# Second attention: part of the sum over keys on TensorE, three buffers of value products, VectorE's sums two steps behind

## The chip, the cores and the metric

The kernel runs on one core of one Trainium2 chip. The metric is the device time of one execution in microseconds (us). Engines are TensorE (PE; its weight loads are listed apart as PEld), VectorE (DVE), ScalarE (ACT), GpSimd (POOL) and SyncE (SP, which only issues transfers here). SBUF is the on-chip memory, PSUM holds TensorE's results in eight banks, named `ps[0]` to `ps[7]`.

## The reference

Two transformer-like blocks on x of shape (8, 512, 256): each has a modulated layer norm, an attention and a mixture of experts. The change lies in the attention of the second block. There every token attends over its own 16 groups of 4 numbers, so scores are 16 by 16 for each row, not token by token:

```python
def shp(t):
    return t.reshape(B * G, H, -1, HD).swapaxes(1, 2)      # H = 16, HD = 4
q, k, v = (shp(q), shp(k), shp(v))
scores = q @ k.swapaxes(-2, -1) * scale
attn = jax.nn.softmax(scores, axis=-1)
o = (attn @ v).swapaxes(1, 2).reshape(B, S, dim)
return o * w.reshape(B, S, dim) @ w_out
```

Each output of `attn @ v` is a sum over 16 keys of an exponential times a value, divided by the sum of the 16 exponentials.

## The kernel before

Every engine has its own program, written out in order in one function each (`vector`, `scalar`, `gpsimd`, `tensor`, `sync`), and semaphores tie them together; nothing is scheduled automatically. The second attention is a loop over `q` from 0 to 63 (`NQ = 64`). Eight consecutive steps belong to one chunk `c = q // 8` of rows. A step handles 2 of 16 query groups for 128 partitions at once: 2 x 16 queries, 16 keys, 4 value numbers each.

What step `q` of each engine's loop does, in the order in which it stands in the program:

- **TensorE**: `less_max(q + 1)` subtracts the row maxima in PSUM (one bf16 matmul, needs VectorE's `top(q + 1)`); `project` computes the heads of a later chunk (6 fp16 matmuls of 256 columns for a head; `heads_at[q]` gives 3 heads in four steps of a chunk, 2 in one or two, 4 in a few early ones) and `turn_qk` regroups them (two turns in each of the two steps `q % 8` = 3 and 4, no heads there); `out_less`; `scores(q + 2)` sums GpSimd's products over the value dimension (4 fp32 matmuls into bank `ps[2 + q % 3]`); then, every second step, `out_project` of a finished tile, and in the others `out_turn`. TensorE starts them strictly in this order.
- **VectorE**: `top(q + 1)` (maximum over keys, L2010), `values(q, 0)` and `values(q, 1)` (exponentials times values: the first product has 16 rows of 64 numbers, of the second VectorE takes the first `vm_cut(q)` = 8 or 9 rows, L1419), `sums(q - 1)` (the sum over the 16 keys, L2032). At the end of a chunk `sums` adds a reciprocal (L2036).
- **ScalarE**: `powers(q + 1)` (exponentials into PSUM for VectorE, L2442), outputs, the copies of the heads out of PSUM (L2081), and last `powers_beside(q + 1)` (exponentials into SBUF for GpSimd and for the denominator, L2449), which waits for VectorE's sums because it writes the buffer that they read.
- **GpSimd**: `products(q + 2)` (query times key, two instructions of 1024 numbers), `values(q)` (the rows of the second product that VectorE leaves), and once a chunk `divide` and `weigh`, all on L2547.

The value products of a step lie in `PV[q % 2]`, laid out `[2 products, 16 queries, 5, 16 keys]`; the five are the 4 value numbers and the exponential itself. `sums` reduces all of it: 160 sums of 16, 2560 numbers read. The heads and the turns share two PSUM banks, `ps[0]` and `ps[1]`, in turn; `pj_free(n)` makes TensorE wait until ScalarE has copied the unit that last used the bank. `vr` counts finished sums, `vm` and `vm_p` finished value products of VectorE and GpSimd, `e_sb` the finished `powers_beside`, `qk` and `qt` the copies of heads and turns.

Of the kernel before, what the change touches and what calls it, by code (L numbers as in the profile page):

```python
# [71 lines left out]
def program(nc, x_in, wqk_in, wv_in, wo_in, rw_in, rb_in, w1_in, w3_in, w2_in, c0_in, m0_in,  # L72
# [3 lines left out]
    with ctx:  # L76
# [428 lines left out]
        def head_unit(c, h):  # L505
            return 12 + 20 * (c - 1) + h if c else h // 2
# [66 lines left out]
        def vm_cut(q):  # L573
            return (8 if q < 16 else 9) if q < 61 else 0
# [250 lines left out]
        def tensor(e):  # L825
# [446 lines left out]
            def pj_free(n):  # L1272

                if n >= 14:
                    c, h = 1 + (n - 14) // 20, (n - 14) % 20
                    if h < 16:
                        pe.wait_ge(s["qk"], heads_copied(c, h))
                    else:
                        pe.wait_ge(s["qt"], 4 * c + h - 15)
                elif n >= 10:  # L1280
                    pe.wait_ge(s["qt"], n - 9)
                elif n >= 2:
                    pe.wait_ge(s["qk"], heads_copied(0, 2 * (n - 2)))
# [131 lines left out]
        def vector(e):  # L1415
# [596 lines left out]
            def values(q, r):  # L2012
# [8 lines left out]
                tt(PV[q % 2][:, r, 0:n, 0:4, :], bc(et[:, 0:n], 2, 4), v[:, 0:n], ALU.mult).then_inc(s["vm"], 1)

            def sums(q):
# [27 lines left out]
            for q in range(NQ):  # L2051
# [25 lines left out]
        def scalar(e):  # L2077
# [342 lines left out]
            def turn_qk(c, bs):  # L2420
                for b in bs:
# [491 lines left out]
```

## Time and profile before

| | us |
|---|---|
| median of 3 runs (1740.03 to 1744.47) | 1744.17 |
| the profiled execution, its own time | 1743.46 |
| its span in the profile | 1741.7 |
| the second attention's loop (first `top` to last sum) | 1082.1 to 1448.2 |

How to read it: the profile covers one execution, 1.8 us of whose time lie outside the span. The loop of the second attention is 366 us of it, with little other work in it but the output tiles of the same attention. A row of the profile's timeline gives start and length; on VectorE and GpSimd records overlap by some tenths of a microsecond, so the time that an instruction takes from its engine is read from one start to the next.

### The profile page before, as it was taken

The numbers are of one execution on the slowest core, as the hardware profiler recorded it, in microseconds if no ns is written. First come the engines' busy times: TensorE is split into PE (matmuls) and PEld (weight loads), VectorE is DVE, ScalarE is ACT, GpSimd is POOL, SyncE is SP. The second block draws the span as 40 slices with busy tenths as digits, with TensorE's granted clock in tenths as the row PEclk, the third lists the DMA queues.
The fourth block names the chain that finished last, engine by engine and source line by source line (L and its number), as shares of the span: only waits on it lengthen the run. The fifth ranks groups of instructions, "written<-read, shape, count | busy, mean of one in ns | idle before, by whom it ended". The sixth has DMA issues, their size and how long they took to land.

```text
span 1741.7 us, 38208 instructions
## 1 busy us (share of the span) xinstructions
PE 1529.0 (88%) x13596; PEld 1145.4 (66%) x13596; DVE 1119.5 (64%) x1777; ACT 909.7 (52%) x2313; POOL 1221.5 (70%) x1024
## 2 busy tenths in 40 slices
PE   6799999986999999999999967877877767699998
PEld 5456666565788888888888853433333326599997
DVE  6778898887334434434444557899999998533332
ACT  5768888853343443433444346545555536344553
POOL 4647777743376776776777727999999996466664
PEclk9899999996799999999999977889999978599999
DMA  6003444419245445444465461011111246388885
GB/s 219 20 30 119 142 135 139 124 35 326 77 96 122 112 108 122 110 110 119 101 186 151 107 188 53 1 28 31 31 43 43 91 152 194 141 259 253 259 262 150
DMA packets 148049, 217.34 MB, mean 125 GB/s; under 512 B 48904, under 2 KB 108576, under 8 KB 142752
## 3 DMA queue, kind: packets, MB, share of 16 engines
q1 hardware_dynamic: 115296, 132.26, 23.6%
q0 software_dynamic: 32576, 82.63, 19.4%
q8 instruction: 122, 2.00, 0.5%
q14 instruction: 55, 0.45, 0.1%
HBM read 143.23 MB, written 71.61 MB: 123 GB/s over the span
## 4 chain that ended last, share of the span: by engine, by line
PE 54%; POOL 20%; DVE 8%; issue 7%; DMA 5%; ACT 1%; POOLq 0%; DVEq 0%; ACTq 0%; SPq 0%
PE ps L829 51%; POOL BIG L2547 16%; DMA BIG<-HB,BIG 5%; DVE BIG L1419 4%; PE ps L946 1%; POOL BIG L2731 1%; POOL BIG L2732 1%; POOL XD L2721 1%; DVE BIG L2032 1%; PE ps L1127 1%; ACT BIG L2081 1%; DVE bnst L1426 1%; POOL BIG L2709 1%; PE ps L1196 0%; POOL out L2721 0%
## 5 line engine op out<-in xcount | busy, mean ns | idle before, releaser
L829 PE MATMUL ps<-BIG 128*128 128x256 f16 (+9 forms) x11168 | 1230.7, 285 | 122.8 <-DVE BIG L2010 49.2
L829 PEld LDWEIGHTS ps<-BIG 128*128 128x128 f16 (+3 forms) x11168 | 940.9, 100 | 382.4 <-DVE BIG L2010 77.8
L2547 POOL TENSOR_TENSOR BIG<-BIG 128x256 f16<-128x256 f32 (+7 forms) x550 | 728.5, 1499 | 221.8 <-ACT BIG L2081 207.6
L2081 ACT ACTIVATE BIG<-BIG 128x512 f16<-128x512 f32 (+3 forms) x527 | 318.1, 661 | 225.5 <-DVE BIG L1419 160.5
L1419 DVE TENSOR_TENSOR BIG<-BIG 128x512 f16<-128x512 f32 (+12 forms) x345 | 258.6, 758 | 209.7 <-ACT BIG L2081 166.6
L2081 ACT ACTIVATE BIG<-ps 128x64 f32<-128x64 f32 (+7 forms) x663 | 232.1, 424 | 210.0 <-PE ps L1127 114.1
L1419 DVE TENSOR_TENSOR BIG<-ps,BIG 128x512 f32<-128x512 f32 (+3 forms) x389 | 285.3, 811 | 13.9 <-PE ps L829 12.5
L1419 DVE TENSOR_TENSOR BIG<-BIG,ps 128x512 f32<-128x512 f32 (+2 forms) x149 | 95.6, 642 | 185.9 <-PE ps L829 160.7
L2032 DVE TENSOR_REDUCE BIG<-BIG 128x160 f32<-128x2560 f32 x64 | 186.5, 2915 | 0.0
L2721 POOL DMA_INDIRECT XD<-BIG x67 | 113.2, 1690 | 85.2 <-DVE BIG L1916 81.4
L2709 POOL DMA_INDIRECT BIG<-HB,BIG x106 | 113.4, 1070 | 50.6 <-issue 26.4
L2155 ACT ACTIVATE BIG<-ps,BIG 128x64 f32<-128x64 f32 x480 | 101.7, 363 | 49.5 <-PE ps L829 49.5
L2721 POOL DMA_INDIRECT out<-BIG x39 | 62.7, 1607 | 60.2 <-DVE BIG L1951 57.6
L2342 ACT ACTIVATE BIG<-ps 128x512 f32<-128x512 f32 x78 | 46.7, 598 | 104.2 <-PE ps L829 98.2
L2295 ACT ACTIVATE BIG<-ps 128x512 f32<-128x512 f32 (+1 forms) x140 | 79.9, 571 | 24.2 <-PE ps L829 20.1
L2731 POOL DMA_INDIRECT BIG<-PT,BIG x67 | 68.3, 1019 | 20.5 <-issue 20.5
L2732 POOL DMA_INDIRECT BIG<-GT,BIG x67 | 66.1, 986 | 20.4 <-issue 20.4
L1916 DVE SCALAR_TENSOR_TENSOR BIG<-ps,BIG 128x256 f32<-128x256 f32 x67 | 32.4, 484 | 71.9 <-PE ps L829 71.7
L2449 ACT ACTIVATE BIG<-ps 128x512 f32<-128x512 f32 x64 | 38.3, 599 | 76.3 <-DVE BIG L2032 76.3
L2442 ACT ACTIVATE ps<-ps 128x512 f32<-128x512 f32 x64 | 37.2, 581 | 54.0 <-PE ps L829 53.8
L829 PE MATMUL ps<-BIG,tri 128*128 128x512 f16 (+1 forms) x264 | 63.1, 377 | 0.9 <-ACT BIG L2108 0.9
L2010 DVE TENSOR_REDUCE BIG<-ps 128x32 bf16<-128x512 f32 x64 | 48.1, 752 | 20.4 <-PE ps L829 20.2
(175 smaller groups left out, 1018.6 us busy)
## 6 DMA issues: line engine op xcount, KB each, us to landing
WD<-BIG SPq DMA_DIRECT2D x80, 256.0 KB
BIG<-in_v SPq DMA_DIRECT2D x32, 512.0 KB
BIG<-in_w SPq DMA_DIRECT2D x24, 512.0 KB
BIG<-WD SPq DMA_DIRECT2D x32, 384.0 KB, 7.7
HB<-BIG SPq DMA_DIRECT2D x64, 128.0 KB, 2.5
WG<-BIG SPq DMA_DIRECT2D x32, 256.0 KB
BIG<-WD SPq DMA_DIRECT2D x16, 512.0 KB, 5.0
XD<-X SPq DMA_DIRECT2D x32, 128.0 KB, 2.5
```

The lines of the kernel that those rows point to most:

```text
L829: return e.matmul(o, lhsT, rhs, start=start, stop=stop, skip_group_check=True)
L1419: return e.tensor_tensor(o, a, b, op)
L2010: e.tensor_reduce(SM[q % 4], shaped(ps[2 + q % 3][:, :], (2, 16, 16)), AX.X, ALU.max).then_inc(s["sm"], 1)
L2032: e.tensor_reduce(OB[c % 2][:, 2 * q2:2 * q2 + 2], PV[q % 2], AX.X, ALU.add).then_inc(s["vr"], 1)
L2081: return e.activation(o, i, ACT.Copy)
L2155: o = e.activation(KVF[i % 2][:, j, 512 + 64 * h:576 + 64 * h], ps[4 + vr_no["v", i, 1] % 2][:, 64 * h:64 * h + 64], ACT.Copy, scale=q[:, ...
L2295: e.activation(m_.UP[u % 2][:, 0:w], ps[2 * u % 4][:, 0:w], ACT.Silu).then_inc(s["su"], 1)
L2547: return e.tensor_tensor(o, a, b, op)
L2709: e.indirect_dma_start(m_.HIN[t % ring], None, m_.HB, bass.IndirectOffsetOnAxis(m_.gi[:, t:t + 1], 0)).then_inc(ld_hi[t % ring], 16)
L2721: e.indirect_dma_start(m_.XD, bass.IndirectOffsetOnAxis(m_.yi[:, t:t + 1], 0), m_.YO[t % 2], None, compute_op=ALU.add).then_inc(st_y[t % 2 ...
L2731: e.indirect_dma_start(m_.PP[:, t:t + 1], None, PT, bass.IndirectOffsetOnAxis(m_.qi[:, t:t + 1], 0)).then_inc(ld_g[t % 3], 16)
L2732: e.indirect_dma_start(m_.G[t % 3], None, GT, bass.IndirectOffsetOnAxis(m_.bi[:, t:t + 1], 0)).then_inc(ld_g[t % 3], 16)
```

## The change

TensorE sums the last 3 or 4 of the 16 keys of a step (3 where it has more than 2 heads to compute in the next step, else 4) with as many fp32 matmuls by the identity, 160 columns each, into the ring `ps[0]`, `ps[1]`. ScalarE copies the 160 sums into the slot of the first of these keys. VectorE's reduction then reads 17 - 3 or 17 - 4 numbers for each sum instead of 16. This holds for steps below `N_SUM = 58`. There is a third buffer of value products, in the space of a weight that is no longer used (`WM1`), `sums` runs two steps behind (`sums(q - 2)`), with two sums in step 60 to catch up, and GpSimd's `divide` and `weigh` move one step later. VectorE takes 11 (first ten steps) or 12 rows of the second product until step 57, GpSimd the other 5 or 4.

```diff
+        PV.append(shaped(WM1.rearrange(FLAT)[:, 0:2560], (2, 16, 5, 16)))
...
+        N_SUM = 58
+        s["ks_ps"], s["ks"] = s["gt"], s["gt_ps"]
+
+        def keys_by_pe(q):
+            if q >= N_SUM:
+                return 0
+            return 3 if len(heads_at[q + 1]) > 2 else 4
+
+        def late_keys(q):
+            return PV[q % 3].rearrange("p r f d k -> p k (r f d)")
+
+        in_turns = [("two", 0, 2 * j) for j in range(8)] + [("turn", 0, b) for b in range(4)]
+        for q in range(NQ):
+            in_turns += [("head", c, h) for c, h in heads_at[q]]
+            in_turns += [("turn", q // 8 + 1, b) for b in turns_next(q)]
+            in_turns += [("keys", q - 1, 0)] if 0 < q <= N_SUM else []
+        unit = {u: n for n, u in enumerate(in_turns)}
+
+        def sums_at(q):
+
+            return {N_SUM + 2: (q - 2, q - 1)}.get(q, (q - 1,) if q > N_SUM + 2 else (q - 2,))
...
-            return (8 if q < 16 else 9) if q < 61 else 0
+            return (11 if q < 10 else 12) if q < N_SUM else 9 if q < 61 else 0
...
+            def sum_keys(q):
+                if not 0 <= q < N_SUM:
+                    return
+                n, first = unit["keys", q, 0], 16 - keys_by_pe(q)
+                pj_free(n)
+                pe.wait_ge(s["vm"], vm_n[q])
+                pe.wait_ge(s["vm_p"], q + 1)
+                pe.wait_ge(s["e_sb"], q + 1)
+                for k in range(first, 16):
+                    m = mm(ps[n % 2][:, 0:160], ident[:, :], late_keys(q)[:, k], k == first, k == 15)
+                m.then_inc(s["ks_ps"], 1)
...
                 turn_qk(q // 8 + 1, turns_next(q))
+                sum_keys(q - 1)
                 for n in out_at(q, O_OUT):
                     out_less(n)
...
-                if q >= 2:
-                    dve.wait_ge(s["vr"], q - 1)
+                if q >= 3:
+                    dve.wait_ge(s["vr"], q - 2)
...
-                e.tensor_reduce(OB[c % 2][:, 2 * q2:2 * q2 + 2], PV[q % 2], AX.X, ALU.add).then_inc(s["vr"], 1)
+                keys, by_pe = 16, keys_by_pe(q)
+                if by_pe:
+                    dve.wait_ge(s["ks"], 1 + q + 1)
+                    keys = 17 - by_pe
+                e.tensor_reduce(OB[c % 2][:, 2 * q2:2 * q2 + 2], PV[q % 3][:, :, :, :, 0:keys], AX.X, ALU.add).then_inc(s["vr"], 1)
...
-                sums(q - 1)
+                for last in sums_at(q):
+                    sums(last)
...
+            def sum_keys(q):
+                if not 0 <= q < N_SUM:
+                    return
+                act.wait_ge(s["ks_ps"], 1 + q + 1)
+                copy(late_keys(q)[:, 16 - keys_by_pe(q)], ps[unit["keys", q, 0] % 2][:, 0:160]).then_inc(s["ks"], 1)
...
-                if q % 8 == 1 and q > 8:
+                if q % 8 == 2 and q > 8:
                     divide(q // 8 - 1)
-                if q % 8 == 2 and q > 8:
+                if q % 8 == 3 and q > 8:
                     weigh(q // 8 - 1)
```

On TensorE, a step with three heads and no projection stood like this before; `sm` is VectorE's `top`, `pm` GpSimd's products, the rows of 128x256 are the heads, those of 32x512 the scores:

```order
L829 MATMUL ps<-BIG 128x512 [waits sm]
L829 MATMUL ps<-BIG 128x256 [waits qk]
L829 MATMUL ps<-BIG 128x256 x5
L829 MATMUL ps<-BIG 128x256 [waits qk]
L829 MATMUL ps<-BIG 128x256 x5
L829 MATMUL ps<-BIG 128x256 [waits qk]
L829 MATMUL ps<-BIG 128x256 x5
L829 MATMUL ps<-BIG 32x512 [waits e_sb,pm]
L829 MATMUL ps<-BIG 32x512 x3
```

Such a step in the changed kernel; `gt_ps` is the semaphore that counts ScalarE's copies of the key sums, the rows of 128x160 are the sums over keys:

```order
L852 MATMUL ps<-BIG 128x512 [waits sm]
L852 MATMUL ps<-BIG 128x256 [waits qk]
L852 MATMUL ps<-BIG 128x256 x5
L852 MATMUL ps<-BIG 128x256 [waits gt_ps]
L852 MATMUL ps<-BIG 128x256 x5
L852 MATMUL ps<-BIG 128x256 [waits qk]
L852 MATMUL ps<-BIG 128x256 x5
L852 MATMUL ps<-BIG,ident 128x160 [waits vm_p,e_sb,vm,qk]
L852 MATMUL ps<-BIG,ident 128x160 x2
L852 MATMUL ps<-BIG 32x512 [waits pm]
L852 MATMUL ps<-BIG 32x512 x3
```

The three matmuls of the key sum now stand between the heads and the scores of the same step, and the second head waits for ScalarE's copy of the key sum of the step before.

On VectorE, steps 60 and 61 before:

```order
L2010 TENSOR_REDUCE BIG<-ps3 128x32 [waits mx_ps,s_ps]
L1419 TENSOR_TENSOR BIG<-ps5,BIG 128x16x64 [waits vr,e_ps]
L1419 TENSOR_TENSOR BIG<-ps5,BIG 128x9x64
L2032 TENSOR_REDUCE BIG<-BIG 128x160 [waits e_sb,vm_p,vm]
L2010 TENSOR_REDUCE BIG<-ps4 128x32 [waits mx_ps,s_ps]
L1419 TENSOR_TENSOR BIG<-ps7,BIG 128x16x64 [waits vr,e_ps]
L2032 TENSOR_REDUCE BIG<-BIG 128x160 [waits e_sb,vm_p,vm]
```

And in the changed kernel (L2045 is the maximum, L1454 the products, L2071 the sum over keys):

```order
L2045 TENSOR_REDUCE BIG<-ps3 128x32 [waits mx_ps,s_ps]
L1454 TENSOR_TENSOR BIG<-ps5,BIG 128x16x64 [waits vr,e_ps]
L1454 TENSOR_TENSOR BIG<-ps5,BIG 128x9x64
L2071 TENSOR_REDUCE BIG<-BIG 128x160 [waits e_sb,vm_p,vm]
L2071 TENSOR_REDUCE BIG<-WM1 128x160 [waits e_sb,vm_p,vm]
L2045 TENSOR_REDUCE BIG<-ps4 128x32 [waits mx_ps,s_ps]
L1454 TENSOR_TENSOR BIG<-ps7,BIG 128x16x64 [waits vr,e_ps]
L2071 TENSOR_REDUCE BIG<-BIG 128x160 [waits e_sb,vm_p,vm]
```

The sums of steps 58 and 59 both stand in step 60 now, with all 16 keys, ahead of the maximum that step 61 begins with.

## Rows read from the trace of the kernel before

**Rows 1.** Busy time: stretch, its us, PE, PEld, DVE, ACT, POOL, granted clock.

```profile
1182.60:1226.10 43.50, 34.84 (x252) 16.72 (x252) 43.05 (x35) 25.23 (x100) 43.50 (x27) 1.00 0.12 31
...
1270.90:1315.60 44.70, 35.70 (x252) 17.14 (x252) 43.05 (x35) 25.32 (x101) 44.70 (x27) 0.96 0.15 42
...
sum 223.10, PE 173.04 PEld 79.95 DVE 215.85 ACT 121.36 POOL 223.10; mean PE 34.61 PEld 15.99 DVE 43.17 ACT 24.27 POOL 44.62
```

**Rows 2.** Timeline of DVE, one regular step (start us, us, engine line op, shapes, count).

```profile
1253.62 0.88 DVE L2010 TENSOR_REDUCE BIG<-ps 128x32 bf16<-128x512 f32 x1
1254.21 2.08 DVE L1419 TENSOR_TENSOR BIG<-ps,BIG 128x1024 f32<-128x1024 f32 x2
1256.01 3.00 DVE L2032 TENSOR_REDUCE BIG<-BIG 128x160 f32<-128x2560 f32 x1
1258.74 0.87 DVE L2010 TENSOR_REDUCE BIG<-ps 128x32 bf16<-128x512 f32 x1
```

**Rows 3.** Timeline of DVE at the end of a chunk.

```profile
1269.27 1.76 DVE L2036 RECIPROCAL BIG<-BIG 128x256 f32<-128x256 f32 x1
1270.94 0.63 DVE L2010 TENSOR_REDUCE BIG<-ps 128x32 bf16<-128x512 f32 x1
```

**Rows 4.** Timeline of POOL in the same steps, three starts.

```profile
1249.66 3.45 POOL L2547 TENSOR_TENSOR BIG<-BIG 128x1024 f32<-128x1024 f32 x2
...
1251.63 3.45 POOL L2547 TENSOR_TENSOR BIG<-BIG 128x448 f32<-128x448 f32 x2
...
1252.73 2.35 POOL L2547 TENSOR_TENSOR BIG<-BIG 128x1024 f32<-128x1024 f32 x1
```

**Rows 5.** Timeline of PE, steps with turns, after GpSimd's divide and weigh.

```profile
1237.65 2.32 PE L829 MATMUL ps<-BIG,ident 32*32 32x512 f32 x16
1241.91 1.41 PE L829 MATMUL ps<-BIG 128*32 128x512 f32 x8 [1.94 <-POOL BIG L2547]
```

**Rows 6.** Who waited for whom, 1270.9 to 1315.6 (us, times, longest).

```profile
PEld ps L829 <- POOL BIG L2547: 5.1, 4, 4.1
```

**Rows 7.** Timeline of PE, one step with three heads and a projection.

```profile
1253.16 0.71 PE L829 MATMUL ps<-ident,BIG 128*128 128x128 f32 x4
1254.55 1.70 PE L829 MATMUL ps<-BIG 128*128 128x512 bf16 x13 [0.69 <-DVE BIG L2010]
1256.57 0.83 PE L829 MATMUL ps<-BIG 128*128 128x256 f16 x6 [0.32 <-ACT BIG L2081]
...
1257.44 1.83 PE L829 MATMUL ps<-BIG 128*32 128x512 f32 x14
...
1259.67 3.66 PE L829 MATMUL ps<-BIG 128*128 128x512 bf16 x27
```

**Rows 8.** Timeline of PE: the last of the four fp32 records.

```profile
1253.59 0.28 PE L829 MATMUL ps<-ident,BIG 128*128 128x128 f32 x1
```

**Rows 9.** Timeline of PE, two steps with four heads, and one with turns.

```profile
1119.13 5.90 PE L829 MATMUL ps<-BIG 128*128 128x512 bf16 x33 [0.81 <-DVE BIG L2010]
1125.85 4.12 PE L829 MATMUL ps<-BIG 128*128 128x512 bf16 x33 [0.82 <-DVE BIG L2010]
...
1108.55 0.39 PE L829 MATMUL ps<-BIG 128*128 128x512 bf16 x1 [0.93 <-DVE BIG L2010]
1108.87 2.32 PE L829 MATMUL ps<-BIG,ident 32*32 32x512 f32 x16
1111.12 1.07 PE L829 MATMUL ps<-BIG 128*32 128x512 f32 x8
```

**Rows 10.** Timeline of DVE, the maximum between those two steps with four heads.

```profile
1125.10 0.69 DVE L2010 TENSOR_REDUCE BIG<-ps 128x32 bf16<-128x512 f32 x1 [1.57 <-PE ps L829]
```

**Rows 11.** Busy time in the two stretches of the 33 matmuls (PEclk: granted clock).

```profile
1119.50:1124.00 4.50, 4.50 (x29) 3.19 (x29) 4.03 (x3) 2.11 (x10) 4.50 (x4) 0.61 0.02 4
1126.00:1130.10 4.10, 3.97 (x33) 2.25 (x31) 4.10 (x3) 2.61 (x13) 4.10 (x4) 1.00 0.00 0
```

**Rows 12.** Timeline of DVE, the maximum of step 62.

```profile
1433.42 0.69 DVE L2010 TENSOR_REDUCE BIG<-ps 128x32 bf16<-128x512 f32 x1 [1.11 <-PE ps L829]
```

More of the change, by code:

```diff
@@ L505, in head_unit @@
         def head_unit(c, h):
-            return 12 + 20 * (c - 1) + h if c else h // 2
+            return unit["head", c, h] if c else h // 2
         def heads_copied(c, h):
@@ L1272, in pj_free @@
             def pj_free(n):
[L1274 to L1283, printed above, removed]
+                if n < 2:
+                    pe.wait_ge(s["gw"], 4)
+                    return
+                kind, c, h = in_turns[n - 2]
+                if kind == "turn":
+                    pe.wait_ge(s["qt"], 4 * c + h + 1)
+                elif kind == "keys":
+                    pe.wait_ge(s["ks"], 1 + c + 1)
                 else:
-                    pe.wait_ge(s["gw"], 4)
+                    pe.wait_ge(s["qk"], heads_copied(c, h))
             def project(c, h):
@@ L1305, in turn_qk @@
                 for b in bs:
-                    n = 20 * c - 8 + 16 + b
+                    n = unit["turn", c, b]
                     pe.wait_ge(s["qk"], heads_copied(c, 15))
@@ L1347, in out_turn @@
                 elif n == N_IN:
+                    pe.wait_ge(s["ks"], 1 + N_SUM)
                     pe.wait_ge(s["qk"], heads_copied(7, 15))
@@ L2427, in turn_qk @@
                         act.wait_ge(s["pm"], pm_p[8 * (c - 2) + 7])
-                    copy(QT[c % 2][:, b].rearrange("p s f h -> p (s f h)"), ps[b % 2][:, :]).then_inc(s["qt"], 1)
+                    copy(QT[c % 2][:, b].rearrange("p s f h -> p (s f h)"), ps[unit["turn", c, b] % 2][:, :]).then_inc(s["qt"], 1)
             def powers(q):
@@ L2446, in powers_beside @@
                     return
-                if q >= 2:
-                    act.wait_ge(s["vr"], q - 1)
-                e.activation(PV[q % 2][:, :, :, 4, :], shaped(ps[2 + q % 3][:, :], (2, 16, 16)),
+                if q >= 3:
+                    act.wait_ge(s["vr"], q - 2)
+                e.activation(PV[q % 3][:, :, :, 4, :], shaped(ps[2 + q % 3][:, :], (2, 16, 16)),
                              ACT.Exp, scale=0.5).then_inc(s["e_sb"], 1)
@@ L2493, in scalar @@
                 turn_qk(q // 8 + 1, turns_next(q))
+                sum_keys(q - 1)
                 for n in out_at(q, O_OUT):
@@ L2827, in values @@
                 pool.wait_ge(s["e_sb"], q + 1)
-                if q >= 2:
-                    pool.wait_ge(s["vr"], q - 1)
+                if q >= 3:
+                    pool.wait_ge(s["vr"], q - 2)
                 v = VT[q // 8 % 3].rearrange("p (f d) k -> p f d k", d=4)
-                tt(PV[q % 2][:, 1, n:16, 0:4, :], bc(PV[q % 2][:, 1, n:16, 4, :], 2, 4), v[:, n:16], ALU.mult).then_inc(s["vm_p"], 1)
+                tt(PV[q % 3][:, 1, n:16, 0:4, :], bc(PV[q % 3][:, 1, n:16, 4, :], 2, 4), v[:, n:16], ALU.mult).then_inc(s["vm_p"], 1)
             def divide(c, part=0):
```

3 lines of the change are left out of this document (2 added, 1 removed).

## The prediction, made blind

> **What bounds the kernel now.** I read the busy table by chunk first. In the five chunks between 1182.6 and 1405.7 GpSimd is busy all of 223.1 us and VectorE 215.9 of them; TensorE shows 173.0 [rows 1]. So two engines are full and a third has a margin that must be read more closely, because the change gives it work.
>
> The timeline of VectorE shows a regular step: maximum at 1253.62, products at 1254.21, sums at 1256.01, next maximum at 1258.74 [rows 2]. That is 0.59 + 1.80 + 2.73 = 5.12 us without a gap. At the end of a chunk comes a reciprocal; from one maximum to the next that step takes 5.12 + 1.96 (the sums begin at 1266.25, 2.73 later would come the next maximum, it comes at 1270.94; in the rows the reciprocal begins at 1269.27 and takes 1.67 of it [rows 3]). Eight steps and a reciprocal are 42.9 us. The chunk in rows 1 took 44.70. The other 1.8 us are one wait: after `divide` and `weigh` GpSimd's products come late, TensorE stands before the scores until 1241.91 [rows 5], and VectorE behind it. The list of waits has TensorE's weight loads waiting for GpSimd for 5.1 us, 4.1 of it in one piece [rows 6]. The chunk before the first of these waits took 43.50 [rows 1], which is the same step without most of it.
>
> **VectorE's part.** The sums read 2560 numbers in 2.73 us, 1.07 ns each. With 3 keys on TensorE they read 2240, with 4 they read 2080: -0.34 and -0.51 us. The products read 1600 numbers in 1.80 us, 1.12 ns each; 3 more rows of 64 cost +0.21 [rows 2]. So a step needs 4.99 or 4.82 us, and a chunk, which has four of each, 1.7 less than before.
>
> **GpSimd's part.** A product takes 1.97 us (1249.66 to 1251.63), its 7 rows of values 1.10 (1251.63 to 1252.73) [rows 4]. Four rows lie between 0.63 (in proportion) and 0.81 (on the line through both); I take 0.72. That is 0.38 less in each step, 3.0 in a chunk, against the 4 us of `divide` and `weigh`. GpSimd needs 5.0 - 0.4 = 4.66 a step, less than VectorE, and the third buffer with `divide` a step later costs it no more than before. I expect the one wait of 1.8 us to go.
>
> If that were all, a chunk would take 44.7 - 1.7 - 1.8 = 41.2 us.
>
> **TensorE's part.** The key sum stands between the heads and the scores. There is a closed loop here: the maximum waits for the scores, `less_max` for the maximum, and the heads, the key sum and the next scores follow in order on TensorE. Its length can be read where it already bound: a run of 33 matmuls (`less_max`, four heads, scores) begins at 1119.13 and takes 5.90, to 1125.03; VectorE's maximum starts at 1125.10, the next `less_max` at 1125.85 [rows 9, 10]. So a step can't be shorter than 0.75 + the run + 0.07. What that gives before the change:
> - Three heads with a projection: `less_max` at 1254.55, scores at 1257.44, and scores last 1.07 [rows 7, 9]: run 3.96, loop 4.78 against the 5.12 that VectorE needs. Slack 0.34.
> - Three heads after a projection: `less_max` comes 0.93 after the maximum (1259.67 less 1258.74) because the projection is still running, run 3.66 [rows 2, 7]: 4.66, slack 0.46.
> - Two turns: 1108.55 to 1111.12, plus 1.07 [rows 9]: run 3.64, loop 4.46, and up to 0.3 more with a projection before it or `out_less` in it.
>
> Price of the key sum: the profile shows an fp32 matmul as two records. Four records of 128 columns start between 1253.16 and 1253.59, 0.143 apart [rows 7, 8]. The trace has none of 160 columns. If the records are not bound by their columns, a matmul costs 2 x 0.143 = 0.29; in proportion to columns it costs 0.36. I take 0.29, because 128 columns are much nearer to 160 than to nothing and the spacing of short records holds a part that does not grow: 0.86 for three keys, 1.15 for four; 0.36 stays as the other end.
>
> The Trainium skill gives another price. "FP8 and Floating Point Precision", section TensorE Precision Notes, says that true FP32 takes four passes through the array; at 2.4 GHz, 160 columns would be an estimated 0.27 us a matmul, 0.80 and 1.07 for a key sum, and by it the chunk below would be 0.4 us shorter. No row here has the width to decide it.
>
> New loops: three heads 4.78 + 0.86 = 5.64 and 4.66 + 0.86 = 5.52, instead of 5.12. Both runs contain waits for ScalarE's copies of the heads (0.32 in the row at 1256.57 [rows 7]); now that VectorE finishes before the loop does, ScalarE starts a step's work earlier against TensorE, so some of it falls away. I take 5.45. Turns: 5.61 to 5.9, taken as 5.75. The step `q % 8` = 2 has two heads and a projection: 3.96 less 0.66 for a head (6 of the matmuls at about 0.11), 1.15 and 0.82 more, 5.3 with the ScalarE wait and 4.95 without it, 5.0. The step `q % 8` = 1 has the reciprocal now and stays VectorE's: 4.99 + 1.95 = 6.94. Sum of a chunk: 4 x 5.45 + 2 x 5.75 + 5.0 + 6.94 = 45.2, against 44.7. Nearly all that VectorE and GpSimd gain goes to TensorE's loop.
>
> **The whole loop.**
> - Steps 24 to 47, three chunks: about 0.4 more each, +1.
> - Steps 16 to 23 had next to no wait for GpSimd to lose: 45.2 against 43.5, +1.7.
> - Steps 0 to 15: four-head steps become 4.94 + 0.86 = 5.8 where they took 5.06, four times +0.75. Against that, the series of matmuls of 5.90 us came after a wait, at a granted clock of 0.61, where the same series at 1.00 took 4.12 [rows 9, 11]; one or two such steps get 1 to 1.8 shorter. Together +1.5.
> - Steps 48 to 55: heads end at step 50, three steps are VectorE's at 4.82: -1.3.
> - Steps 56 to 59: no heads, VectorE's at 4.8, and the last wait for GpSimd goes: -2.5.
> - Steps 60 to 63: the doubled sums bring +2.73, of which the wait of 1.11 in step 62 [rows 12] and some others take up half: +1.2.
>
> Sum +1.6 us. With the lower price of the key sum, or with ScalarE's waits gone altogether, it is -3. I take -1. The profiled execution, 1743.46, is 0.7 below the median; from the median 1744.17 this is 1743 us. A difference under 0.3%, 5 us, can't be told from none here.
>
> ScalarE gets one copy of 160 columns, about what it pays for a copy of a head, ahead of `powers_beside`; that one waited for VectorE's sums anyway. The copy and the reduction that reads it are a step apart. Cover gone, it costs 0.3 us a step.
>
> **The rivals.**
> 1. VectorE stays the bound: TensorE's runs shrink, by ScalarE's waits and a cheap key sum, below 4.99. For it: TensorE's busy time is only 35.7 of 44.7 in a chunk [rows 1]. Against it: the busy share says nothing of a loop with 0.3 to 0.5 us slack that gets 0.86. Halfway there (loops of 5.2 and 5.5, chunk 43.9) six chunks give -8, 1735 us; all the way, 41.2 a chunk, about -20, 1724.
> 2. Slower: the key sum costs 0.36 us a matmul, in proportion to its columns, and ScalarE's waits stay. Three heads 5.8, turns 6.0, the two-head step 5.5: with 6.94 a chunk is 47.6. Against 44.7 that is +2.9 over the four and a half chunks in which heads are computed, 1757 us. It decides from 0.32 us a matmul on. For it: the records at 1253.16 and after include weight loads that wider columns may not hide.
> 3. The clock: TensorE's waits for GpSimd go, and with them the stretches at half clock (1.2 GHz); the granted clock was 0.96 over the chunk in rows 1. A mean of 0.96 means 8% of the chunk, 3.6 us, at half clock, so up to 1.8 us of TensorE's time a chunk comes back, and as TensorE's loop is now the bound, it shows: 45.2 - 1 a chunk, -5 more, 1737 us. The Trainium skill, "TensorE: Matmul & The Clock Gate", Part 1: The HAM clock gate, says that the default state is throttled and that activity releases it, so a busier TensorE should run warmer; rows 11 agree on the two levels. Against it: the series at half clock lie right behind the waits, mostly in steps that had slack or that I have counted.
> 4. The new copy holds up ScalarE, and `powers_beside` becomes late: +0.3 a step in 58 steps, 1760. Little speaks for it, as ScalarE is busy 25 of 44.7 us.
>
> **Chances.** My forecast 0.42, of which 0.06 ends above +5 us; rival 1 0.22; rival 3 0.14; rival 2 0.16; rival 4 0.04; 0.02 for no effect at all. Faster by over 0.3% comes from rivals 1 and 3: 0.36. Slower: rivals 2 and 4 and 0.06 of the first, 0.26. Within 0.3%: 0.38. The forecast's own range is 1738 to 1750; taken out to rival 1 short of VectorE's bound and to rival 2 it is 1729 to 1756.
>
> **What would show it.** The 128x160 fp32 records on TensorE give the price: 3 of them 0.86, 4 of them 1.15 from the start of the first to the start of the scores. The maximum should wait for TensorE in most steps, three-head steps should be 5.4 to 5.5 apart, the turn steps 5.7 to 5.8; the sums should take 2.4 and 2.2. GpSimd should have gaps, and its wait of 1.9 at the scores should be gone. I am wrong if the maxima stand 4.8 to 5.0 apart in three-head steps: then VectorE is still the bound.

## The result, and the profile after

| | median us | ratio to before, 95% interval |
|---|---|---|
| before, 5 runs (1740.03 to 1744.47) | 1741.35 | |
| after, 5 runs (1804.29 to 1808.71) | 1805.29 | 1.037 [1.0356, 1.0383] |
| predicted | 1743 (1729 to 1756) | |

The changed kernel is slower by 3.7%, far above the predicted range. Its profiled execution took 1808.56 us, with a span of 1806.8. The whole loss lies in the second attention: from the first maximum to the last the loop takes 418.6 us (1080.09 to 1498.71) where it took 351.3 (1082.09 to 1433.42), 67.3 more, against 65.1 in the span.

The page of the profile after: busy time, the chain that ended last, and three of the costliest groups.

```profile
PE 1635.2 (91%) x14006; PEld 1224.2 (68%) x14006; DVE 1107.0 (61%) x1777; ACT 928.4 (51%) x2371; POOL 1195.5 (66%) x1024
...
PE 69%; DVE 11%; POOL 6%; issue 4%; DMA 4%; ACT 3%; POOLq 0%; DVEq 0%; ACTq 0%; SPq 0%
...
L852 PE MATMUL ps<-BIG,ident 128*128 128x160 f32 (+1 forms) x534 | 125.1, 779 | 6.8 <-ACT BIG L2121 6.1
...
L2071 DVE TENSOR_REDUCE BIG<-BIG 128x160 f32<-128x2080 f32 (+2 forms) x43 | 105.9, 2462 | 0.0
...
L2045 DVE TENSOR_REDUCE BIG<-ps 128x32 bf16<-128x512 f32 x64 | 43.8, 684 | 97.1 <-PE ps L852 97.1
```

The last row is the one to read first. Ahead of the maxima VectorE now stands idle for 97.1 us over the 64 steps, all of it put down to TensorE. TensorE has 69% of the chain that ended last, where it had 54% before.

One chunk (eight steps) in the busy table, the one that answers to the 44.70 us of [rows 1]:

```profile
core 0: us, PE busy (x) PEld busy (x) DVE busy (x) ACT busy (x) POOL busy (x), PEclk, DMA share, GB/s
1299.36:1354.07 54.71, 51.85 (x310) 28.48 (x309) 42.18 (x33) 27.98 (x108) 42.26 (x26) 0.94 0.13 35
```

A chunk takes 54.7 us, ten more. VectorE and GpSimd have become lighter, as the change meant; TensorE, with 35.7 us before, shows 51.9. The timeline of TensorE in two three-head steps, which answer to [rows 7], the first without and the second with `out_less`:

```profile
1342.60 2.66 PE L852 MATMUL ps<-BIG 128*128 128x512 bf16 x19
1345.09 1.78 PE L852 MATMUL ps<-BIG,ident 128*128 128x160 f32 x6
1346.81 1.06 PE L852 MATMUL ps<-BIG 128*32 128x512 f32 x8
1347.80 0.71 PE L852 MATMUL ps<-ident,BIG 128*128 128x128 f32 x4
1348.69 2.58 PE L852 MATMUL ps<-BIG 128*128 128x512 bf16 x19 [0.17 <-DVE BIG L2045]
1351.11 1.79 PE L852 MATMUL ps<-BIG,ident 128*128 128x160 f32 x6
```

Three key-sum matmuls are six records of 160 columns, from 1345.09 until the scores start at 1346.81: 1.72 us where 0.86 was forecast. Record by record the starts are 0.271 us apart, so a matmul costs 0.54 us and not 0.29. VectorE's timeline over these steps:

```profile
1341.64 0.69 DVE L2045 TENSOR_REDUCE BIG<-ps 128x32 bf16<-128x512 f32 x1 [3.23 <-PE ps L852]
1342.25 2.08 DVE L1454 TENSOR_TENSOR BIG<-ps,BIG 128x1024 f32<-128x1024 f32 x2
1344.25 2.31 DVE L2071 TENSOR_REDUCE BIG<-WM 128x160 f32<-128x2080 f32 x1
1347.94 0.69 DVE L2045 TENSOR_REDUCE BIG<-ps 128x32 bf16<-128x512 f32 x1 [1.38 <-PE ps L852]
```

VectorE is through long before the next maximum may start: 6.30 us a step (1341.64 to 1347.94), 1.38 of them waiting, against 5.12 without a gap in [rows 2]. The sums over keys cost what the prediction said (2.31 for 2080 numbers).

The turn steps lost most, they take 8.45 and 8.58 us now. TensorE in the first, and behind the dots the key sum of the second:

```profile
1325.58 0.38 PE L852 MATMUL ps<-BIG 128*128 128x512 bf16 x1
1325.89 2.22 PE L852 MATMUL ps<-BIG,ident 32*32 32x512 f32 x16
1328.71 2.42 PE L852 MATMUL ps<-BIG,ident 128*128 128x160 f32 x8 [0.61 <-ACT BIG L2121]
1331.06 1.93 PE L852 MATMUL ps<-BIG 128*32 128x512 f32 x8
...
1337.40 2.42 PE L852 MATMUL ps<-WM,ident 128*128 128x160 f32 x8 [0.70 <-ACT BIG L2121]
```

And ScalarE, which copies the turns:

```profile
1328.06 1.09 ACT L2121 ACTIVATE BIG<-ps 128x512 f32<-128x512 f32 x2 [1.11 <-PE ps L852]
```

Three things stand in these rows. The key sum follows two turns in the ring of two banks, so it waits for ScalarE's copy of the first turn, and that copy starts only at 1328.06, when TensorE is done with both. The key sum then takes 2.35. And the scores, which take 1.07 in [rows 9], take 1.93 here, with the granted clock down to 0.50, the 1.2 GHz level (PEclk, the third number from the end):

```profile
1328.71:1331.05 2.34, 2.34 (x8) 1.53 (x8) 0.99 (x1) 0.44 (x1) 2.34 (x2) 0.96 0.76 196
1331.06:1333.07 2.01, 2.01 (x10) 0.34 (x9) 0.01 (x1) 1.65 (x6) 1.60 (x2) 0.50 0.75 177
...
1337.40:1339.90 2.50, 2.50 (x9) 2.05 (x9) 1.01 (x1) 0.48 (x2) 0.08 (x1) 0.56 0.00 0
```

### The profile page after: what moved, and what is told of

The parts are those of the page before. It is cut to its first block, busy times and chain, and to the rows that moved or that the text cites. A ratio compares the mean times of both kernels' runs of the same rounds, so it can differ in the third digit from the quotient of the medians.

```text
span 1806.8 us, 39194 instructions
## 1 busy us (share of the span) xinstructions
PE 1635.2 (91%) x14006; PEld 1224.2 (68%) x14006; DVE 1107.0 (61%) x1777; ACT 928.4 (51%) x2371; POOL 1195.5 (66%) x1024
## 4 chain that ended last, share of the span: by engine, by line
PE 69%; DVE 11%; POOL 6%; issue 4%; DMA 4%; ACT 3%; POOLq 0%; DVEq 0%; ACTq 0%; SPq 0%
PE ps L852 66%; DVE BIG L1454 4%; DMA BIG<-HB,BIG 3%; POOL BIG L2594 3%; ACT BIG L2121 2%; DVE BIG L2071 2%; PE ps L969 1%; DVE BIG L2045 1%; PE ps L1150 1%; POOL XD L2768 1%; ACT ps L2482 1%; POOL BIG L2778 1%; POOL BIG L2779 1%; DVE bnst L1461 1%; POOL BIG L2756 0%
## 5 line engine op out<-in xcount | busy, mean ns | idle before, releaser
L2594 POOL TENSOR_TENSOR BIG<-BIG 128x256 f16<-128x256 f32 (+7 forms) x529 | 691.6, 1336 | 279.6 <-ACT BIG L2121 213.6
L1454 DVE TENSOR_TENSOR BIG<-BIG 128x512 f16<-128x512 f32 (+12 forms) x345 | 256.0, 750 | 210.0 <-ACT BIG L2121 167.9
L2121 ACT ACTIVATE BIG<-ps 128x64 f32<-128x64 f32 (+8 forms) x702 | 250.6, 425 | 258.4 <-PE ps L852 116.6
L1454 DVE TENSOR_TENSOR BIG<-ps,BIG 128x512 f32<-128x512 f32 (+2 forms) x348 | 248.8, 781 | 13.8 <-PE ps L852 12.4
L1454 DVE TENSOR_TENSOR BIG<-BIG,ps 128x512 f32<-128x512 f32 (+2 forms) x149 | 95.7, 642 | 189.7 <-PE ps L852 159.4
L852 PE MATMUL ps<-BIG,ident 128*128 128x160 f32 (+1 forms) x534 | 125.1, 779 | 6.8 <-ACT BIG L2121 6.1
L2071 DVE TENSOR_REDUCE BIG<-BIG 128x160 f32<-128x2080 f32 (+2 forms) x43 | 105.9, 2462 | 0.0
L2045 DVE TENSOR_REDUCE BIG<-ps 128x32 bf16<-128x512 f32 x64 | 43.8, 684 | 97.1 <-PE ps L852 97.1
L2382 ACT ACTIVATE BIG<-ps 128x512 f32<-128x512 f32 x78 | 46.6, 598 | 104.1 <-PE ps L852 100.7
L852 PEld LDWEIGHTS ps<-BIG,ident 128*128 128x128 f32 (+1 forms) x534 | 59.6, 165 | 48.4 <-ACT BIG L2121 31.6
```

Of the source, the lines that this page charges most:

```text
L852: return e.matmul(o, lhsT, rhs, start=start, stop=stop, skip_group_check=True)
L1454: return e.tensor_tensor(o, a, b, op)
L2045: e.tensor_reduce(SM[q % 4], shaped(ps[2 + q % 3][:, :], (2, 16, 16)), AX.X, ALU.max).then_inc(s["sm"], 1)
L2071: e.tensor_reduce(OB[c % 2][:, 2 * q2:2 * q2 + 2], PV[q % 3][:, :, :, :, 0:keys], AX.X, ALU.add).then_inc(s["vr"], 1)
L2121: return e.activation(o, i, ACT.Copy)
L2594: return e.tensor_tensor(o, a, b, op)
```

## The experiments

The question was why the same fp32 matmul that showed 0.143 us a record for 128 columns [rows 8] took 0.271 for 160. What differs besides the width is how the moving operand lies in SBUF: the key sum reads one key of `[16 queries, 5, 16 keys]`, 160 numbers 64 bytes apart. Theory A says that the step costs TensorE half its rate. The kernel before ran again beside each experiment, with medians from 1736.85 to 1744.87, so only ratios to it are compared. Step and chunk times are worked out from the starts of the maxima; a chunk is the fifth, steps 32 to 39, unless another is named.

**e1_close: TensorE reads the same amount, adjacent.** This kernel, e4_strides, e5_keys_turns and e7_close_after leave the last 3 or 4 keys out of the attention.

```diff
-            return PV[q % 3].rearrange("p r f d k -> p k (r f d)")
+            return ...rearrange("p (k n) -> p k n", k=16) if by == "pe" else ...
```

> The changed kernel, but TensorE's key sum reads 160 numbers that lie next to each other instead of 160 that lie 64 bytes apart (other numbers of the same buffer), and ScalarE multiplies its copy by 0, so the last 3 or 4 keys are missing from the attention. Number and size of all instructions stay. Theory A (the 64 byte step halves the rate at which TensorE reads the moving operand): records of the key sum 0.13 to 0.14 us apart instead of 0.27, a chunk 28 x 2 x 0.135 = 7.6 us shorter, 54.7 to 47.1, time about 1755. Theory B (each fp32 record pays for its weight load on top of its columns): records stay at 0.27, time stays at 1805.

Measured: ratio 1.0088 [1.0068, 1.0108]. Records 0.136 apart instead of 0.271. TensorE in a turn step:

```profile
1296.61 1.35 PE L852 MATMUL ps<-BIG,ident 128*128 128x160 f32 x8 [0.51 <-ACT BIG L2121]
1297.89 1.07 PE L852 MATMUL ps<-BIG 128*32 128x512 f32 x8
```

Its chunk and its scores in the busy table:

```profile
1269.93:1316.43 46.50, 42.58 (x310) 24.54 (x309) 42.11 (x33) 28.90 (x109) 41.86 (x26) 1.00 0.14 41
1297.89:1299.03 1.14, 1.14 (x10) 0.30 (x10) 0.01 (x1) 1.03 (x4) 1.14 (x2) 1.00 0.83 214
```

Theory A holds, and time and chunk are as expected: one changed step of one operand gives back 8.2 of the 10 us a chunk, 1.4 of them by way of the clock (worked out below). In this chunk the granted clock stays at 1.00 and the scores take 1.07 again, though the engine waits nearly as long ahead of the key sum. It doesn't stay there everywhere: one turn step of the chunk of steps 16 to 23 took 8.15 us, and there eight adjacent records took as long as strided ones:

```profile
1208.43 2.50 PE L852 MATMUL ps<-BIG,ident 128*128 128x160 f32 x8 [0.66 <-ACT BIG L2121]
```

```profile
1208.43:1210.73 2.30, 2.30 (x9) 2.18 (x9) 1.14 (x1) 0.44 (x1) 2.20 (x2) 0.50 0.00 0
```

**e4_strides: 4, 8, 16 and 32 bytes in successive chunks.** One run, as e1_close otherwise.

```diff
+            step = (1, 2, 4, 8)[q // 8 % 4]
+            return ...[:, 0:160 * step * (16 // step)].rearrange("p (k n s) -> p k n s", n=160, s=step)[:, :, :, 0]
```

> As the run with adjacent numbers (ScalarE's copy times 0), but the step of the 160 numbers that TensorE reads is 4, 8, 16 and 32 bytes in chunks 0 and 4, 1 and 5, 2 and 6, 3 and 7. Theory A: records 0.13 apart at 4 bytes and 0.27 from some step on, which the run is to tell. Theory B: 0.27 in all chunks.

Measured: 1774.94 us in one run. TensorE's key sums of four keys at 4, 8, 16 and 32 bytes:

```profile
1109.74 1.35 PE L855 MATMUL ps<-BIG,ident 128*128 128x160 f32 x8 [0.50 <-ACT BIG L2124]
...
1144.80 1.40 PE L855 MATMUL ps<-BIG,ident 128*128 128x160 f32 x8
...
1186.14 2.51 PE L855 MATMUL ps<-BIG,ident 128*128 128x160 f32 x8
...
1241.48 2.56 PE L855 MATMUL ps<-BIG,ident 128*128 128x160 f32 x8
```

Medians of the spacing between records are 0.136, 0.142, 0.284 and 0.290 us (0.271 at 64 bytes in the changed kernel). Between 8 and 16 bytes the spacing doubles, and beyond it hardly changes: a cliff and not a slope. That 64 bytes came out a little cheaper than 32 is not explained.

**e2_kmajor: keys outermost in the buffer, everything computed.**

```diff
-        PV = area.ring(2, 2, 16, 5, 16)
+        PV = area.ring(2, 16, 2, 16, 5)
...
+        PV = [v.rearrange("p k r f d -> p r f d k") for v in PV]
```

> The changed kernel with the value products laid out with the key outermost ([16 keys, 2, 16, 5] in memory instead of [2, 16, 5, 16 keys]); everything computed as before. TensorE then reads 160 adjacent numbers, VectorE, ScalarE and GpSimd write with a step of 640 bytes and VectorE's sum reads with that step. Theory A: records 0.13 to 0.14 apart and about 1755, if the other engines do not care for the step. Theory B: 1805. A third result: the other engines pay for the step, VectorE's sum longer than 2.3 to 2.5 us, and the time over that of the run with adjacent numbers and scrap data.

Measured: ratio 1.0825 [1.0793, 1.0857], the third of the results that the expectation names. TensorE's records are 0.136 apart for the most part, but VectorE's groups became dear, against 2476 ns for the same sum after the change, and TensorE waited for it:

```profile
L2072 DVE TENSOR_REDUCE BIG<-BIG 128x160 f32<-128x2240 f32 x17 | 69.9, 4113 | 0.0
```

```profile
1320.48:1383.60 63.12, 48.62 (x308) 27.36 (x308) 62.55 (x35) 31.35 (x108) 43.43 (x26) 0.89 0.11 30
```

The step that was taken from TensorE was given to VectorE, 640 bytes between two keys, and VectorE pays as well: sums of 2240 numbers 4.1 us instead of 2.5, products of 1024 numbers 2.10 instead of 1.26.

**e3_no_pe: three buffers and the lag alone.** No key sum, VectorE's rows as before.

```diff
-            if q >= N_SUM:
-                return 0
+            return 0
             return 3 if len(heads_at[q + 1]) > 2 else 4
...
-            return (11 if q < 10 else 12) if q < N_SUM else 9 if q < 61 else 0
+            return (8 if q < 16 else 9) if q < 61 else 0
```

> Three buffers, sums two steps behind, divide and weigh a step later, but no key sum on TensorE and none on ScalarE, VectorE's sums over all 16 keys and its 8 or 9 rows of the second product as in the kernel before. If the key sum is the whole loss: VectorE bound at 5.12 a step, 1738 to 1745, with GpSimd's wait of 1.9 a chunk at most partly gone because GpSimd needs 5.04 a step as before. If the lag or the third buffer costs by itself: 1750 or more.

Measured: ratio 0.9995 [0.9983, 1.0008]. This part is neutral, so the loss comes with the key sum. The wait for GpSimd's products stayed, in smaller pieces:

```profile
PEld ps L850 <- POOL BIG L2589: 3.7, 5, 1.5
```

Against 5.1 us, 4.1 of it at once [rows 6]. The doubled sums make one step at the end 7.85 us long (5.13 before), but the next and the one ahead of it get shorter.

**e5_keys_turns: e1_close with the key sum ahead of the turns.**

```diff
-                turn_qk(q // 8 + 1, turns_next(q))
                 sum_keys(q - 1)
+                turn_qk(q // 8 + 1, turns_next(q))
```

> As the run with adjacent numbers (same part of the keys left out), but in the two steps of a chunk with turns the key sum stands ahead of the turns instead of behind them, on TensorE and ScalarE. Theory: behind the turns the key sum waits for ScalarE's copy of the first turn, which starts only when both turns are done; ahead of them it waits for nothing. Turn steps 5.7 us instead of 6.5, 13 or so of them: 1744 against 1754.5. Rival: the turn steps are long because of the turns and the key sum themselves: 1754.

Measured: ratio 1.0051 [1.0033, 1.0069]; turn steps 6.35 where e1_close had 6.52 and 6.58. The expectation of 5.7 failed. The wait for a copy changed its place: by the order in the ring the second turn now needs the copy of the key sum, and from the start of the turns to the scores it takes 2.72 us instead of the 2.25 of [rows 9].

**e6_after_scores: the changed kernel with the key sum behind the scores.** Everything computed, 64-byte step.

```diff
-                sum_keys(q - 1)
                 for n in out_at(q, O_OUT):
                     out_less(n)
                 if q:
                     scores(q + 2)
+                sum_keys(q - 1)
```

> The changed kernel with the key sum behind the scores instead of ahead of them (ScalarE's copy behind its copy for the output). All is computed. Theory: the loss lies in the closed loop from scores to maximum to less_max, not in TensorE's total; about 0.9 us behind the scores were idle in every second step and the turn steps' wait for ScalarE falls there too. Three-head steps alternate around 5.3 and 6.2 instead of 6.13 and 6.30, turn steps 5.3 to 6.5 instead of 8.5: 1755 to 1765. If TensorE's total were the bound instead, the place would not matter: 1805.

Measured: ratio 1.0225 [1.0204, 1.0246], chunk 51.58. The direction is right (3.1 us a chunk less than after), the size was overestimated. The turn steps came near what was expected (6.80 and 6.47 for an expected 5.3 to 6.5, instead of 8.45 and 8.58) and the two-head step fell from 6.03 to 4.83, but the three-head steps, expected at 5.3 and 6.2, took 6.4 to 6.9, more than the 6.1 to 6.3 after the change. With TensorE busy 48.8 of the 51.6 us the engine itself is nearly full, so little more is to be had by moving work inside its program.

```profile
1280.85:1332.43 51.58, 48.76 (x309) 28.36 (x310) 42.07 (x34) 27.44 (x108) 41.66 (x27) 1.00 0.13 37
```

**e7_close_after: both, adjacent and behind the scores.** The edits of e1_close and e6_after_scores.

> Both: adjacent numbers (last 3 or 4 keys left out, ScalarE's copy times 0) and the key sum behind the scores. 0.8 us of key sum fit into the 0.9 us in which TensorE waits for the maximum, so steps without projection are VectorE's at 4.8 to 5.0, those with one 5.0 to 5.3; a chunk 42 to 43.5: 1725 to 1735, faster than the kernel before. If ScalarE's later copy or the buffer ring holds it up: 1740 or more.

Measured: ratio 0.9983 [0.9969, 0.9997], below the expected gain; it is the other outcome that the expectation names, a hold-up by ScalarE's copy. Turn steps fell to 5.2 and the two-head step to 4.76, but three-head steps stayed at 5.59 to 5.90: TensorE's loop sets them still, and in it stands a wait for ScalarE ahead of the third head:

```profile
1299.30 0.83 PE L852 MATMUL ps<-BIG 128*128 128x256 f16 x6 [0.98 <-ACT BIG L2121]
```

**e8_rows10: e3_no_pe with 10 rows for VectorE.**

```diff
-            return (8 if q < 16 else 9) if q < 61 else 0
+            return 10 if q < 61 else 0
```

> No key sum, three buffers and sums two steps behind, and VectorE takes 10 rows of the second product in all steps below 61 (before 8 or 9), GpSimd 6. All is computed. Theory: with 5.04 us a step plus 4 a chunk GpSimd sets the chunk's 45 us; VectorE 5.19 a step and 43.5 a chunk, GpSimd 4.92 a step: the chunk 43.6, time 1728 to 1732. Rival: VectorE is the bound already: 61 rows of 0.07, 1741.

Measured: ratio 0.997 [0.9958, 0.9982], between the two expectations; steps 5.19, and one of 6.00 a chunk; chunks 44.1 to 44.7 in the middle of the loop. The step of 6.00 does not wait for GpSimd. It is the one behind the reciprocal: TensorE has stood idle for 3.58 us for VectorE's maximum, the granted clock is 0.50 in the whole step, the 13 matmuls take 3.17 us where they take 1.70 in [rows 7], and the next maximum waits 0.79 us for the scores:

```profile
1275.44 3.17 PE L850 MATMUL ps<-BIG 128*128 128x512 bf16 x13 [3.58 <-DVE BIG L2041]
1280.75 0.69 DVE L2041 TENSOR_REDUCE BIG<-ps 128x32 bf16<-128x512 f32 x1 [0.79 <-PE ps L850]
```

```profile
1274.75:1280.75 6.00, 5.31 (x23) 2.28 (x24) 5.21 (x5) 2.76 (x10) 5.83 (x4) 0.50 0.00 0
```

**e9_some_keys: the key sum only where VectorE is late.** Everything computed, 64-byte step, 4 keys in one step of eight and in the headless end.

```diff
-            return 3 if len(heads_at[q + 1]) > 2 else 4
+            return 4 if (q + 1) % 8 == 1 or q >= 52 else 0
...
+            return (11 if q % 8 in (2, 3, 4) else 10) if q < 61 else 0
```

> The changed kernel, all of it computed, with TensorE's key sum (of 4 keys) only in one step of eight, the one behind the turns' last, and in the headless end, and VectorE at 11 rows in the three steps behind it and 10 elsewhere below step 61. Theory A (a key-sum matmul at a 64-byte step costs TensorE 0.54 us, and it pays only where TensorE had a wait to give): one step a chunk takes 8 x 0.54 = 4.3 us more of TensorE; put where VectorE is late, it costs a chunk nothing and lets VectorE and GpSimd catch up some 0.6 to 1.1 us a chunk, chunks of 43.3 to 43.8 us beside 44.4 without any key sum: ratio 0.993 to 0.995. Rival (TensorE has no free 4.3 us even there): chunks of 45 us or more, ratio 0.998 to 1.005.

Measured: ratio 0.9958 [0.9944, 0.9972]. The chunk takes 43.83, about as expected. The step of 6.00 in e8_rows10 takes 4.70, but not for the reason that the expectation gives, work taken from VectorE and GpSimd alone: 0.50 of the difference is VectorE's sum of 2080 instead of 2560 numbers (2.31 and 2.81 us), and 0.79 is the wait for TensorE, which is gone. The key sum fills a part of the time in which TensorE stood idle, 1.02 us are left of the 3.58, and the granted clock is 1.00:

```profile
1275.01 1.70 PE L853 MATMUL ps<-BIG 128*128 128x512 bf16 x13 [1.02 <-DVE BIG L2046]
```

```profile
1274.33:1279.02 4.69, 4.00 (x30) 2.25 (x30) 4.69 (x5) 2.06 (x9) 4.54 (x4) 1.00 0.01 3
```

No run fills the gap without lightening the sum, so the two parts are read from the rows and not tested apart. The ratio falls a little short of what was expected, and its interval overlaps that of e8_rows10 (0.9958 to 0.9982 there), so the gain of 4.1 us between the two loops (348.6 and 344.5 from first to last maximum) is seen in the profiles and not settled by the times.

```profile
1256.58:1300.41 43.83, 38.47 (x266) 18.82 (x265) 43.72 (x34) 25.90 (x101) 43.68 (x28) 0.96 0.14 43
```

**e10_two_keys: 2 keys in every step.**

```diff
-            return 3 if len(heads_at[q + 1]) > 2 else 4
+            return 2
```

> The changed kernel, all of it computed, with TensorE summing 2 keys in every step instead of 3 or 4. Theory A (0.54 us a matmul, TensorE's loop sets the step): 28 x 2 = 56 matmuls a chunk of eight steps become 32, a run is 1 to 2 heads x 2 fewer; per step 3 or 4 keys x 2 halves = 6 or 8 matmuls become 4, so 2 to 4 fewer, about 24 a chunk x 0.27 us a record pair's half or 0.54 a matmul: 6.5 us a chunk at least, from 54.7 to about 48, time about 1762 (ratio 1.010 to 1.015). Rival (what costs is the key sum's being there at all, its wait for the power copies and ScalarE's copy behind it): little changes, 1790 or more, ratio above 1.027.

Measured: ratio 1.0233 [1.0216, 1.025], between the two expectations. Three-head steps take 5.59 and 5.76 where they took 6.13 and 6.31: 0.54 and 0.55 for the one matmul fewer. The rest falls short, because VectorE with 12 rows and 15 numbers needs 5.15 (two-head step 5.09 instead of 6.03, 0.94 for two matmuls; in four other chunks that step took 5.73 to 5.91, at a mean granted clock of 0.70), and because of turn steps like the second of these, where the scores of the same program ran at a lower granted clock:

```profile
1258.41:1259.55 1.14, 1.14 (x10) 0.30 (x10) 0.00 (x1) 1.03 (x4) 1.14 (x2) 1.00 0.94 230
1306.22:1307.96 1.74, 1.74 (x10) 0.28 (x9) 0.00 (x0) 1.59 (x6) 1.74 (x2) 0.59 0.87 221
```

The first turn step of the chunk was 6.50 us in the one case and 7.11 in the other, 0.6 apart, and the scores show all of it.

**e11_pairs: two keys adjacent, an 8-byte step for TensorE, everything computed.** Three keys on TensorE in every step, VectorE three of four value numbers of the second product.

```diff
-        PV = area.ring(2, 2, 16, 5, 16)
+        PV = area.ring(2, 8, 2, 5, 16, 2)
...
+            return PV[q % 3].rearrange("p r d f a b -> p a b (r d f)")
...
+                    m = mm(ps[n % 2][:, 0:160], ident[:, :], late_keys(q)[:, k // 2, k % 2], k == first, k == 15)
```

> The changed kernel, all of it computed, with the value products laid out in pairs of keys: eight pairs outermost, and inside each the 160 numbers with their two keys adjacent. TensorE then reads one key at a step of 8 bytes; VectorE and GpSimd write and read two adjacent numbers and then step 1280 bytes. TensorE sums 3 keys in every step, VectorE takes three of the four value numbers of the second product (as much as 12 rows) below step 61, and ScalarE writes the exponentials for GpSimd in two instructions instead of one. Theory (an operand runs at full rate if two reads in a row fall within 16 bytes, on TensorE and on VectorE): key-sum records 0.142 us apart, VectorE's sums of 2240 numbers 2.4 to 2.6 us as before, chunks 45.5 to 46.5 us, ratio 1.003 to 1.010. Rival (what VectorE pays for is any large step inside the operand, also when two numbers are adjacent): sums of 3.9 us and more, chunks above 55 us, ratio above 1.05.

Measured: ratio 1.0121 [1.0097, 1.0146], two thousandths above the expected end; the chunk is 47.6 us, 1.1 above the expected 46.5. The mechanism is as expected on both engines: records 0.142 us apart, and VectorE reads pairs 1280 bytes apart at the old price:

```profile
L2072 DVE TENSOR_REDUCE BIG<-BIG 128x160 f32<-128x2240 f32 x24 | 59.9, 2496 | 0.0
```

2496 ns beside 4113 in e2_kmajor and 2476 after the change. The miss lies in the turn steps again, 6.11 and 7.87 in this chunk. In the second the scores ran at 0.50 granted clock:

```profile
1302.00:1304.30 2.30, 2.30 (x11) 0.33 (x10) 0.00 (x0) 1.17 (x4) 1.79 (x2) 0.50 0.00 0
```

**e12_pairs_after: the same, with the key sum behind the scores.** The edit of e6_after_scores.

> The kernel with pairs of keys, all of it computed, with the key sum behind the scores instead of ahead of them. Theory (with the cheap read TensorE's loop is the last bound, and behind the scores the key sum leaves the part of the loop that the maximum waits for): the turn steps fall to 5.2 to 5.4 us and the step behind them to 4.8 to 5.1, chunks of 44.5 to 45.5 us, ratio 0.996 to 1.001. Rival (the order doesn't matter once the read is cheap): the same as with the key sum ahead of the scores, within 0.2%.

Measured: ratio 0.9978 [0.9967, 0.9989], as expected, with turn steps of 5.0 and a two-head step of 4.93. This is the whole change with its read mended and its key sum moved, and it is faster than before, by 0.2%. What holds it is one wait in each three-head step, here in the last row, 0.97 us ahead of the third head:

```profile
1249.47:1294.21 44.74, 40.95 (x301) 23.90 (x302) 42.04 (x33) 27.67 (x116) 41.77 (x27) 1.00 0.15 42
```

```profile
1256.36 1.69 PE L853 MATMUL ps<-BIG 128*128 128x512 bf16 x13
1259.02 0.83 PE L853 MATMUL ps<-BIG 128*128 128x256 f16 x6 [0.97 <-ACT BIG L2122]
```

The bank of that head is not emptied by ScalarE in time. Three-head steps take 5.6 to 5.9.

## Why the prediction was wrong

**The step that failed** is the price of the key sum: "I take 0.29 ... 0.36 stays as the other end." Measured: 0.54 us a matmul, beyond both ends. The number 0.143 was read from matmuls whose moving operand, the identity, is adjacent; I weighed width against width and never asked how the 160 numbers lie. The diff says it, in `rearrange("p r f d k -> p k (r f d)")`, a step of 16 numbers. The upper bound was taken on the wrong property. e1_close and e4_strides show this step alone to be the cause of the doubled price, and e10_two_keys shows the price by the dose. Of the 3.7% e1_close gives back 2.8 (1.037 to 1.0088); most of the rest lies in the turn steps, below.

The Trainium skill states the rule, in "Advanced Engine Details and Errata", section SBUF Cachelines: lines are 16 bytes, and at least two reads must fall on one line for full performance. The runs agree: 8 bytes full rate, 16 bytes half (0.142 and 0.284 us), and with pairs VectorE full rate again. The prediction cited another page of the Trainium skill, whose four passes for true FP32 made an estimated 0.27 us a matmul ("FP8 and Floating Point Precision", TensorE Precision Notes); with adjacent numbers that is what the runs show, 2 x 0.136.

The prediction's own sum of a chunk, beside the fifth chunk:

| steps | predicted | after | e1_close |
|---|---|---|---|
| four with three heads, each | 5.45 | 6.22 | 5.41 |
| two with turns, together | 11.5 | 17.03 | 13.1 |
| the one with two heads | 5.0 | 6.03 | 4.97 |
| the one with the reciprocal | 6.94 | 6.79 | 6.79 |
| chunk | 45.2 | 54.7 | 46.5 |

- **The loop** "0.75 + the run + 0.07" was right, and so were its lengths: with the key sum at 0.27 a matmul (e1_close) three of the four rows come out within 0.15. Rival 2 named the right place and direction; its 0.36 and its 1757 us were too small by the same error.
- **Turn steps** had a second error: the 1.6 us between 11.5 and 13.1 are there without the strided read. Each waits for ScalarE's copy of the first turn (0.51 to 0.70 us on TensorE), since the key sum is the third user of two banks. The prediction counted that wait for heads only. Those waits are 1.1 to 1.3 of the 1.6; the rest isn't resolved. What lies between 13.1 and 17.0 is 8 matmuls by 0.27, 2.2, and the lower clock, 0.87 in one step and 0.54 in the other (from the scores to the maximum 2.00 and 1.67 instead of 1.13), 3.6 of 3.9. That the strided read itself brings the lower clock on is not shown.
- **VectorE and GpSimd** were right: sums of 2.48 and 2.3 us, 4.82 in the steps without heads, the reciprocal step 6.79, GpSimd 42.3 of 54.7 us a chunk. GpSimd's wait at the scores went as forecast: TensorE's waits for it in the chunk are 1.6 us, the longest 0.4, where they were 5.1 and 4.1.
- **The third rival, the clock**, did not come to pass where it was priced: TensorE became busier (35.7 to 51.9 us of a chunk) and the granted clock was 0.94 instead of 0.96. In the third chunk, steps 16 to 23, it fell from 1.00 to 0.94, in the first two it rose, from 0.80 to 0.86 and from 0.81 to 0.88, and over the whole loop it is 0.90 before and 0.91 after. So a busier TensorE had no steadily higher clock here. The two levels for which rival 3 names [rows 11] can't be read from them, since 0.61 is a mean; 0.50 stands in the rows above. What it describes, a wait cut short and the clock back at 1.00, shows in e8_rows10 and e9_some_keys.
- **The fourth, ScalarE's copy,** cost nothing in the steps with heads: `less_max` and three heads stand in one row without a wait (1342.60 and 1348.69 above).
- **The end of the loop** came about as forecast. For the doubled sums the forecast was +1.2 us: the last two distances between maxima are 7.84 and 4.46 where they were 5.13 and 5.65, +1.5, and +0.9 if the last sum is taken as the end. For steps 56 to 59 it was -2.5: they take 21.1 instead of 24.1 us, -3.0, 1.60 of it a wait of VectorE that is gone.
- **Two sums are off by a little** and decide nothing: the chunk of rival 1 adds up to 43.7 and not 43.9, and by the price of four passes the chunk would be 0.5 us shorter and not 0.4.

## What to carry to other kernels

Ahead of pricing a matmul or a reduction from another row, compare the step of the operands and not only their size: with fp32 numbers 16 to 64 bytes apart TensorE needed twice the time here, and VectorE's sum took 1.65 times as long with 640 bytes between its numbers (nothing shorter was tried for it). A layout with two numbers adjacent served both. Where several engines read one buffer in different orders, look for the layout that gives each two neighbours, before giving one of them the adjacent numbers. And work that is moved to an engine with idle time costs its full length if it lands inside the loop that the others wait for; behind the scores the same key sum cost 3 us a chunk less. Last, work can also pay in a gap by keeping the clock up: read the granted clock of a step that is long without a reason.

## What the runs showed of the hardware

- The step of TensorE's fp32 moving operand: 0.136, 0.142, 0.284 and 0.290 us a record of 160 columns at 4, 8, 16 and 32 bytes, 0.271 at 64.
- The strided read showed no dependence on the granted clock: eight records took 2.42 us at 0.96 and 2.42 at 0.56 in the rows above. The adjacent one depends on it: eight records took 1.35 us at 1.00 and 2.50 at 0.50 in e1_close. So the half rate looks like a limit of the read and not of the array; no run here changes the clock alone.
- Low clock without a long wait: after 2.2 us of turns, 0.6 us of waiting and 2.35 us of strided key sum the granted clock stood at 0.50. With adjacent reads it stood at 1.00 behind the same turns and wait in most turn steps of e1_close and fell to 0.50 in the one shown. e10_two_keys had both outcomes for one program, so what decides is open.
- Low clock behind a wait: in each of five chunks of e8_rows10 TensorE stood idle for 3.58 us, and the granted clock of the step behind it was 0.50; in e9_some_keys 1.02 us were left of that wait and the clock was 1.00. In e10_two_keys the same step, behind 1.88 us of waiting, had 1.00 in one chunk and about 0.70 in four.
- ScalarE's copy of the first turn began only when TensorE had finished both (1328.06). Why it isn't released after the first eight matmuls is open.
